# Sorting row numbers instead of rows in a one-core attention and expert kernel

## The reference, cut to what matters

```python
xn = layernorm(x)                                    # 4096 tokens x 256
# differential attention, causal, 8 heads, two score maps for each head
q, k, v = xn @ wq.T, xn @ wk.T, xn @ wv.T
attn = softmax(q1 k1) - lmbda * softmax(q2 k2)       # 1024 x 1024 for each head
s = rmsnorm(attn @ v) * (1 - L_INIT) @ wo.T
# mixture of experts, E = 8, TOP_K = 2
logits = xn @ router_weight.T + router_bias
top_vals, top_idx = top_k(logits, 2); top_w = softmax(top_vals)
gate, up = split(xn @ gate_up_proj[e] + gate_up_bias[e])
act = (clip(up) + 1) * min(gate, 7) * sigmoid(1.702 * min(gate, 7))
ffn = sum over the two experts of top_w * (act @ down_proj[e] + down_bias[e])
out = x + s * silu(ffn)
```

## Time and profile before

| | |
|---|---|
| median of 3 runs | 1129.12 us (1128.27 to 1133.16) |
| the profiled execution | 1129.73 us |
| its span, first to last instruction | 1127.9 us |
| PE busy | 945.8 us (84%) |
| DVE busy | 937.6 us (83%) |
| ACT busy | 776.0 us (69%) |
| POOL busy | 222.6 us (20%) |
| DMA moved | 178.11 MB, mean 158 GB/s |

### The profile page before, as it was taken

The page is one execution under the profiler, slowest core; times in us unless marked ns, Lnnn a source line. Parts: engine busy times, 40 slices in busy tenths (PEclk is TensorE's granted clock), DMA queues, the critical chain, the costliest instruction groups (busy, mean ns, idle before and its releaser), DMA issues. The chain is left out here.

```text
span 1127.9 us, 25764 instructions
## 1 busy us (share of the span) xinstructions
PE 945.8 (84%) x6626; PEld 662.2 (59%) x6627; DVE 937.6 (83%) x1873; ACT 776.0 (69%) x1982; POOL 222.6 (20%) x427
## 2 busy tenths in 40 slices
PE   5889875899999899898998988967999999963665
PEld 4777653666666666666666666644555555532544
DVE  6677667999999999999999999954777777754886
ACT  3544245999999999999999999962333333325563
POOL 2000000132222222222222222220000000017771
PEclk9999985999999999999999999998999999986677
DMA  7999965768777686775756657401222222223563
GB/s 260 353 359 335 330 258 146 160 163 202 171 173 165 158 204 170 178 160 117 165 128 137 155 119 166 99 20 59 79 80 84 79 79 83 79 92 95 168 184 104
DMA packets 92410, 178.11 MB, mean 158 GB/s; under 512 B 11744, under 2 KB 50144, under 8 KB 91360
## 3 DMA queue, kind: packets, MB, share of 16 engines
q1 hardware_dynamic: 74336, 147.38, 48.9%
q0 software_dynamic: 7680, 20.98, 6.5%
q10 hardware_dynamic: 10368, 9.44, 2.5%
HBM read 108.56 MB, written 69.21 MB: 158 GB/s over the span
## 5 line engine op out<-in xcount | busy, mean ns | idle before, releaser
L1049 DVE TENSOR_REDUCE nmax<-bank 128x1 f32<-128x1024 f32 (+3 forms) x256 | 259.8, 1015 | 4.2 <-PE bank L881 4.1
L982 ACT ACTIVATE Pr_long<-bank,nmax 128x1024 f32<-128x1024 f32 (+3 forms) x256 | 252.1, 985 | 11.0 <-DVE nmax L1049 10.8
L1009 ACT COPY AT<-bank 128x512 f32<-128x512 f32 (+3 forms) x384 | 177.1, 493 | 3.8 <-PE bank L920 1.8
L879 PE MATMUL bank<-Ks_first,Qs_first 128*128 128x512 f32 (+3 forms) x384 | 124.2, 413 | 31.1 <-ACT Pr_short L996 19.8
L996 ACT ACTIVATE Pr_short<-bank,nmax 128x128 f32<-128x128 f32 (+3 forms) x256 | 138.4, 541 | 8.9 <-DVE nmax L1067 1.7
L1241 PE MATMUL bank<-gu_sb,xsT 128*128 x288 | 139.8, 609 | 4.7 <-DVE hid L1358 0.5
L920 PE MATMUL bank<-ident,Pr_long 128*128 128x128 f32 x832 | 127.4, 280 | 18.1 <-DVE Pr_long L1099 18.0
L1099 DVE SCALAR_TENSOR_TENSOR Pr_long<-Pr_long,coef 128x1024 f32<-128x1024 f32 (+3 forms) x128 | 137.3, 1073 | 0.0
L879 PE MATMUL bank<-Ks_second,Qs_second 128*128 128x512 f32 (+3 forms) x384 | 119.4, 400 | 18.4 <-ACT Pr_short L996 18.1
L881 PE MATMUL bank<-maskb,identb 128*128 128x128 bf16 x512 | 118.1, 233 | 0.0
L920 PEld LDWEIGHTS bank<-ident,Pr_long 128*128 128x128 f32 x832 | 90.4, 142 | 31.4 <-issue 27.3
(11 more groups left out here) (147 smaller groups left out, 1634.5 us busy)
## 6 DMA issues: line engine op xcount, KB each, us to landing
q_parts<-PARTS SPq DMA_DIRECT2D x32, 512.0 KB, 5.1
k_parts<-PARTS SPq DMA_DIRECT2D x32, 512.0 KB, 3.7
Qs_first<-q_parts SPq DMA_DIRECT2D x64, 256.0 KB
Ks_first<-k_parts SPq DMA_DIRECT2D x64, 256.0 KB
Qs_second<-q_parts SPq DMA_DIRECT2D x64, 256.0 KB, 6.1
Ks_second<-k_parts SPq DMA_DIRECT2D x64, 256.0 KB, 7.0
xs_dram<-zeros SPq DMA_DIRECT2D x8, 1152.0 KB, 7.4
xs<-xs_dram SPq DMA_DIRECT2D x72, 128.0 KB, 2.0
```

The lines of the kernel that those rows point to most:

```text
L879: nc.tensor.matmul(at[:, c0:c1], Qs[head][:, m, q * P:(q + 1) * P], Ks[head][:, m, c0:c1], start=True, stop=(c1 < N))
L982: nc.scalar.activation(long_probs(p)[:, m, 0:N], long_slot[m][:, 0:N], ACT.Exp, bias=nmax[:, 4 * p + m:4 * p + m + 1], scale=1.0, accum_ou ...
L1009: nc.scalar.copy(AT[u % 6][:, 0:w], tb[u % BANKS][:, 0:w]).then_inc(unit_out, 1)
L1049: nc.vector.tensor_reduce(nmax[:, 4 * p + m:4 * p + m + 1], long_slot[m][:, 0:N], AX.X, ALU.max, negate=True).then_inc(long_maxed, 1)
```

## The change

- In stage 1 the stores of zeros to `xs_dram` are gone. In their place a table of 9216 row numbers, `ids_dram`, is filled once (36 KB) with numbers of rows past the end. `PARTS` has eight buffers in place of four. DVE's routing is cut to the counts and the list of experts; it copies the two sums out of PSUM to SBUF, and the running sum and the product that make `slot_of` go to POOL, into the first iteration of attention (`route`, 14 steps in frames 0 to 4).
- In stage 2 POOL loads no rows. In iterations 1 to 8 it scatters row numbers of 4 bytes (token + 4096 for the second expert), 8 indirect DMAs of 128 numbers in an iteration, and waits for the landing of the ones before at the start of the next. After the tenth iteration SP reads the table back by one DMA whose runs are single words (`slot_rows`, 128 partitions x 72). In the last iteration POOL makes token numbers of it and gathers the first tile of rows. The routing's scratch lies in the space of `gub_sb`, so SP loads the experts from the third on only when POOL's 14 steps are done.
- In stage 3 POOL gathers each tile of rows from `xn_dram` (`rows_in`, up to five tiles ahead in its list, held by `xs_turned`) and scatters each tile of results to `y_dram` (`results_out`), which is in token order, one half for each expert. SP's loads and ACT's stores are gone. The waits for the last scatters stand at the end of the block.
- In stage 4 SP loads the results with two plain DMAs of 512 KB for a chunk (`load_y`); POOL's 64 gathers are gone.
- The blocks of all four stages are opened with `no_gpsimd_drain=True`.

```diff
-            PARTS = [sb(f"PARTS{i}", [P, 2, CH], F32R, where=ph) for i in range(4)]
+            PARTS = [sb(f"PARTS{i}", [P, 2, CH], F32R, where=ph) for i in range(QKT)]
...
-            with nc.Block() as block:
+            with nc.Block(no_gpsimd_drain=True) as block:
...
                     def chunk(b, h):
-                        sp.dma_start(xs_v[b * 2 + h], zeros[:]).then_inc(zeros_stored, 16)
...
-                            act.wait_ge(parts_stored[i % 4], 16 * (4 * b + 2 * h + i // 4 + 1))
+                            act.wait_ge(parts_stored[i], 16 * (2 * b + h + 1))
...
+                    dve.wait_ge(ranks_bank, 1)
+                    nc.vector.tensor_copy(pre, bank6[:, 0:NT * E].rearrange("p (t e) -> p t e", e=E))
+                    nc.vector.tensor_copy(tot, bank7[:, 0:NT * E].rearrange("p (t e) -> p t e", e=E))
...
+                    then(nc.vector.tensor_reduce(tokens, bank7[:, 0:NT * E].rearrange("p (t e) -> p e t", e=E), AX.X,
+                                                 ALU.add))
...
+                    sp.wait_ge(routed, ROUTE_OPS)
+                    with sp.Fori(FREE_EXPERTS, E) as it:
...
+                    with sp.Fori(E, SORT_ITS + 2) as it:
+                        for u in range(2):
+                            load(it + 1, u)
+                    sp.wait_ge(ids_sorted, 16 * SORT_ITS * NP)
+                    with nc.allow_non_contiguous_dma("one word of each slot"):
+                        sp.dma_start(slot_rows[:], ids_dram.rearrange("(n p) o -> p (n o)", p=P)
+                                     ).then_inc(rows_known, 16)
...
+                    def route(p):
+                        if p == 0:
+                            tokens_before()
+                            double(0, 1)
+                            double(1, 2)
+                        if p == 1:
+                            double(0, 4)
+                            double(1, 8)
+                            double(0, 16)
...
+                        for n in SORT_AT.get(p, ()):
+                            i, k = n // TOP_K, n % TOP_K
+                            pool.indirect_dma_start(ids_dram, bass.IndirectOffsetOnAxis(sort_slot[:, i, k:k + 1], 0),
+                                                    sort_id[:, i, k:k + 1], None).then_inc(ids_sorted, 16)
...
+                @block.gpsimd
+                def _(pool):
+                    def rows_in(n):
+                        pool.wait_ge(xs_turned, seen(n // 2 - 1, n % 2))
+                        pool.indirect_dma_start(xs[n % 2][:], None, xn_dram, bass.IndirectOffsetOnAxis(
+                            slot_tokens[:, n:n + 1], 0)).then_inc(xs_loaded[n % 2], 16)
+                    def results_out(n):
+                        pool.wait_ge(y_ready, seen(n // 2, n % 2))
+                        pool.indirect_dma_start(y_dram, bass.IndirectOffsetOnAxis(slot_rows[:, n:n + 1], 0),
+                                                ys[n % 2][:], None).then_inc(y_stored[n % 2], 16)
...
+                    for n in range(2, AHEAD):
+                        rows_in(n)
+                    for n in range(SLOT_TILES):
+                        if n + AHEAD < SLOT_TILES:
+                            rows_in(n + AHEAD)
+                        results_out(n)
+                    for u in range(2):
+                        pool.wait_ge(y_stored[u], 16 * (NIT3 + 1))
...
-                        store(it, n - 1)
...
+                    def load_y(b, h):
+                        for k in range(TOP_K):
+                            sp.dma_start(yg[h][:, :, k, :], y_v[k, b, h]).then_inc(y_loaded[h], 16)
...
                     with sp.Fori(0, B - 1) as b:
                         for h in range(2):
+                            sp.wait_ge(ff_ready, credited(b, 2, h))
+                            load_y(b + 1, h)
                             store(b, h)
...
-                            for i in range(CT):
-                                for k in range(TOP_K):
-                                    pool.indirect_dma_start(
-                                        yg[h][:, i, k, :], None, ys_dram,
-                                        bass.IndirectOffsetOnAxis(yslot[h][:, i, k:k + 1], 0)
-                                    ).then_inc(y_gathered[h], 16)
```

More of the change, by code:

```diff
@@ L501, in _ @@
-                    nc.vector.memset(run[0][:, 0:1, :], 0.0)
-                    then(nc.vector.tensor_copy(run[0][:, 1:NT, :], tot[:, 0:NT - 1, :]))
-                    src, span = 0, 1
-                    while span < NT:
-                        nc.vector.tensor_copy(run[1 - src][:, 0:span, :], run[src][:, 0:span, :])
-                        then(nc.vector.tensor_tensor(run[1 - src][:, span:, :], run[src][:, span:, :],
-                                                     run[src][:, 0:NT - span, :], ALU.add))
-                        src, span = 1 - src, 2 * span
+                    tokens, tiles, first, end, first_slot = (per_e[:, i] for i in range(5))
@@ L509, in _ @@
+                    then(nc.vector.tensor_reduce(tokens, bank7[:, 0:NT * E].rearrange("p (t e) -> p e t", e=E), AX.X,
+                                                 ALU.add))
                     low_parts(B - 1, 1, range(QKT // 2, QKT // 2 + 2))
-                    tokens, tiles, first, end, first_slot = (per_e[:, i] for i in range(5))
-                    then(nc.vector.tensor_tensor(tokens, run[src][:, NT - 1, :], tot[:, NT - 1, :], ALU.add))
-                    ce = cmp[:, 0:E * NT].rearrange("p (e t) -> p e t", e=E)
+                    ce = rcmp[:, 0:E * NT].rearrange("p (e t) -> p e t", e=E)
@@ new lines, in then, with tokens_before @@
+                    def then(ins):
+                        ins.then_inc(routed, 1)
+                        steps[0] += 1
+                        pool.wait_ge(routed, steps[0])
+                    first_slot = per_e[:, 4]
+                    ck = rcmp[:, 0:TOP_K * NT * E].rearrange("p (k t e) -> p k t e", k=TOP_K, e=E)
+                    def tokens_before():
+                        nc.gpsimd.memset(run[0][:, 0:1, :], 0.0)
+                        then(nc.gpsimd.tensor_copy(run[0][:, 1:NT, :], tot[:, 0:NT - 1, :]))
@@ L1321, in act_out @@
                                    ).then_inc(act_T_ready, 1)
-                def store(it, n):
-                    if not there(it, n):
-                        return
-                    it, u = it + n // 2, n % 2
-                    nc.scalar.wait_ge(y_ready, seen(it, u))
-                    nc.scalar.dma_start(ys_v[it, u], ys[u][:]).then_inc(y_stored[u], 16)
                 @block.scalar
                 def _(act):
-                    for u in range(2):
-                        act.sem_inc(y_stored[u], 16)
                     for s in (xsT_ready, tanh_ready, act_T_ready):
```

273 lines of the change are left out of this document (157 added, 116 removed).

## The result

The changed kernel takes 1137.49 us (median of 7 runs, 1131.59 to 1140.89), the kernel before beside it on the same chip 1128.4 us. The ratio is 1.0068, with a 95% interval of 1.0041 to 1.0094: slower by 0.7%, where 1092.5 was forecast.

What follows compares the result with a forecast made beforehand. Bounds: transfers in mid-stage 1, DVE and ACT in stage 2, PE in stage 3, POOL in stage 4. From 1129.73 us, -11.4 - 4.1 + 0.5 - 6.5 + 0.5 - 16.2 = -37.2 gave 1092.5; range 1081 to 1110.

Steps and rivals of the forecast that it cites:

- Stage 2: Attention: eight number scatters an iteration and POOL's 14 steps fit beside the other work; cost 0.5 us, bounds 0 and 5.
- the table's read holds up attention: Rival, attention: reading the table back takes 32 us, 11 over its room on SP's queue, giving 1103.5; chance 0.14.
- Stage 1 and its end: Stage 1: no zero stores and eight buffers save 11.4 us; DVE's shorter routing at the end saves 4.1.
- with eight buffers to even out the rest: Stage 1: without 9.4 MB of zeros, transfers fall just under PE and DVE, buffers covering the rest; 11.4 us together.
- Into stage 3: From attention's end to stage 3's first product: without POOL's drain, 5.2 us in place of 11.9; gain 6.5 (3 to 8).
- Stage 3: Stage 3: POOL's gather and scatter for each tile stay hidden under its 3.36 us; small end effects together +0.5 us.
- The rival that POOL becomes its bound: Stage 3: POOL's DMA instructions exclude DVE's SBUF work, 4.2 us a tile, 1155 in all; chance 0.04, milder lag 0.10.
- Stage 4: Stage 4: plain loads start it 8.4 us earlier, DVE-bound chunks of 10.9 us save 7.8; gain 16.2 (10 to 18).

Runs made afterwards that it cites:

- the first experiment: The changed kernel without its 64 scatters of row numbers, GpSimd adding to the semaphore itself, table filled with 0 to 9215: 1085.5 us, ratio 0.9605.
- after: The changed kernel itself, with the whole change made to the kernel before: 1137.49 us, ratio 1.0068.
- the eighth experiment: The kernel before with its row scatters replaced by four 4-byte scatters an iteration to a packed 36 KB table: 1130.9 us, ratio 1.0005.
- The eleventh experiment: The changed kernel with table words 512 bytes apart, cleared word by word, and four PARTS buffers in place of eight: 1098.4 us, ratio 0.9721.

## Why the prediction was wrong

**The step that failed** is "*Stage 2* ... Number scatters are 8 an iteration at 1.03 us and 0.3 to 0.5 of gap, at most two in a frame. Cost: I take 0.5 us, bounds 0 and 5". It measured 53.0. The instructions were priced rightly (64 of 1019 ns, and nobody waited for GpSimd's time), but only as time of the engine that issues them. Their writes were given no price: 8192 words of 4 bytes are 0.03 MB. Yet I had the clue in hand. In "the table's read holds up attention" I asked what 9216 small packets do to a queue, for the read. The read cost nothing, as forecast: it is issued at 572.8 us, and the 1.3 us of iteration 9 lie before 557; in the first experiment, which reads the same packed table, that iteration has 35.5 us. I did not ask it of the writes that fill the same table. The bounds of 0 and 5 had no row under them: the kernel before has no indirect DMA with rows shorter than 1 KB, and an operation without such a row needed wider ones.

What stood in its place is shown as far as this: the loss needs words that lie 4 bytes apart in DRAM (64 bytes apart: no loss), written by scatters, and many to one table (four an iteration: none; eight to two tables: 10 us; eight to one: 51). In the 8 us looked at, packets of the loads took 0.99 us on average in place of 0.26, and a packet of instructions 1.8 in place of 0.6. Loads of K come late in after, and engines stand still together; that they do so for instructions is not shown. The Trainium skill has a rule that fits how this reaches the engines ("DMA: Bandwidth & Descriptors", section "Queues, rings and completion order"): a transfer's semaphore goes up only after all earlier writes of the same DMA engine have landed, those of other queues too. No run here separates that from plainly slow packets. Open are: why two tables differ so much from one, which property of the table's place gives 14 to 15 us, and why a packed scatter takes 6.3 us to land (the eighth experiment's median) where a row scatter of before takes 3.0.

**Stage 1 and its end**: forecast -15.5, measured -18.2 (attention starts at 159.83 in place of 177.98). The waits of after in 14 to 158 us and two rows of PE's timeline:

```profile
ACT PARTS L599 <- PE bank L667: 45.4, 58, 2.6
```

```profile
53.48 7.34 PE L667 MATMUL bank<-XNT_parts,wqk_parts 128*128 128x512 f32 x24 [2.28 <-DVE PARTS L460]
...
159.83 1.19 PE L970 MATMUL bank<-Ks_first,Qs_first 128*128 128x512 f32 x2 [8.14 <-ACTq L1113]
```

ACT waits for PE and no longer for stores, the waits behind `rank` stayed as said (2.28 us where 2.36 was), and the last idle time fell from 10.43 to 8.14. The size was about right. I laid the waits to the 9.4 MB of zeros first, "with eight buffers to even out the rest". The eleventh experiment seems to turn this round: with four buffers attention starts at 172.12 us, 13 later than with eight. But 9 of these 13 us come from its clear, as shown there. Without them the buffers are worth some 4 us and the zeros, with the shorter end of the stage, some 14: the zeros come first, as the prediction had it. Both are estimates; the run that would show it, four buffers in after itself, was not made.

**Into stage 3**: forecast -6.5, measured -7.7. The drain is worth 6.5 us over all four blocks, 5.7 of it here; I had ascribed 7.5. The timelines of after:

```profile
790.53 0.24 POOL L844 COPY VO<-Ob 128x64 f32<-128x64 f32 x1 [0.38 <-ACT Ob L1131]
791.41 0.97 POOL L1279 DMA_INDIRECT xs_second<-xn_dram,slot_tokens  x1 [0.65 <-SPq L1264]
...
795.01 5.29 PE L1345 MATMUL bank<-gu_sb,xsT 128*128 x8
```

4.2 us from the last copy to the first product, where 5.2 was laid out.

**Stage 3**: forecast +0.5, measured -4.2; I did not look for these 4.2 us, and no experiment tells where they come from. The rival that POOL becomes its bound is refuted. GpSimd's two indirect DMAs a tile by line, and DVE's work beside them by line in 800 to 1000 us:

```profile
L1276 POOL DMA_INDIRECT y_dram<-ys,slot_rows x72 | 71.4, 992 | 41.7 <-DVE ys L1489 40.5 <-issue 1.2
L1270 POOL DMA_INDIRECT xs_first<-xn_dram,slot_tokens x35 | 33.9, 969 | 23.7 <-PE bank L1331 19.6 <-issue 4.1
```

```profile
L1477 DVE SCALAR_TENSOR_TENSOR act_in<-up,glu 128x256 f32<-128x256 f32 x63 | 26.8, 425 | 9.0 <-DVE up L1471 6.1
L1459 DVE TENSOR_SCALAR hid<-hid 128x256 f32<-128x256 f32 x63 | 18.5, 294 | 2.1
```

They take 0.99 and 0.97 us, and DVE's instructions 425 and 294 ns, the very figures of the earlier trace rows, where GpSimd was idle. In time they do overlap:

```profile
814.29 0.97 POOL L1270 DMA_INDIRECT xs_first<-xn_dram,slot_tokens  x1 [0.49 <-PE bank L1331]
814.67 0.29 DVE L1459 TENSOR_SCALAR hid<-hid 128x256 f32<-128x256 f32 x1
```

70 of the 72 `act_in` instructions overlap an indirect DMA. By the rule of the Trainium skill ("SBUF — State Buffer", section "Who interferes with whom") a DVE instruction with two inputs in SBUF contends with one of GpSimd that reads SBUF. Here 141 indirect DMAs stood in the stage, and neither side got longer.

**Stage 4**: forecast -16.2, measured -15.0. (The prediction's 75.5 us should read 75.2: 9.8 and 6 x 10.9.) ACT's first work in it and DVE's second and third chunk:

```profile
1038.11 1.70 ACT L1667 ACTIVATE ff<-yg,yw 128x256 f32<-128x256 f32 x4 [4.22 <-DMA yg<-y_dram]
...
1049.24 1.67 DVE L1740 SCALAR_TENSOR_TENSOR ff<-yg,yw,ff 128x256 f32<-128x256 f32 x4 [2.35 <-ACT ff L1667]
1060.27 1.67 DVE L1740 SCALAR_TENSOR_TENSOR ff<-yg,yw,ff 128x256 f32<-128x256 f32 x4
```

The rows are used 5.5 us after the stage starts (13.7 before), and a chunk takes 11.0 us by DVE; 10.9 was said.

Of the range, 1081 to 1110 would have held the kernel with its words apart (1085.9 to 1086.8 in three forms), which is also the version that beats both: 4% under before and, by the medians, 4.5% under after. That the rest of the sum was sound is no excuse for the missing term.

## What to carry to other kernels

Price a scatter by its writes as well as by its issue, and give a tiny table in DRAM some room: one entry for each 64 bytes made 51 us of difference here for 0.55 MB of space. When a stage grows and no engine has more work, look at packets and bytes of each DMA queue beside its share: a queue that is full and moves a third of its usual bytes may be held up by another, and the culprit's own row can read 0.3%. And before an edit with small writes is costed at nothing, look for one row of the trace with writes that small; without one the range must say so.

## What the runs showed of the hardware that was not expected

- Words of 4 bytes that lie next to each other in DRAM were written at half the pace of words 64 or 512 bytes apart: 33.3 against 17.1 and 16.4 us to landing, median of two transfers of 4608 words, by a plain DMA.
- With many such words scattered to one table, packets of other queues took 0.99 in place of 0.26 us, and a packet of instructions 1.8 in place of 0.6.
- The kernel's loss is steep in the number: 0 us for four scatters an iteration, 51 for eight; and 10 for eight over two tables. In packet time of the loads' queue the same three cost 9, 51 and 25 us.
- A table declared elsewhere or made longer gave 14 to 15 us back with the same writes.
- 141 indirect DMAs of GpSimd beside DVE's work on SBUF left both at their durations (0.97 and 0.99 us; 425 and 294 ns).
- The drain of GpSimd at the end of four blocks: 6.5 us, 5.7 of them at one place.
